# Attention kernel on one core: queries held once in steps of 28, and 112 rows of scores in place of 128

## The reference

```python
x = x + attention(layernorm(x))     # 16 heads of 128, 4 key/value heads, wq, wk, wv, wo
x = x + int8_linear(layernorm(x))   # weights and activations rounded to 8 bits, plus bias
# in attention, for each head:
scores = q @ k.T / sqrt(128)
mask = (k_pos <= q_pos) & ((k_pos < 4) | (k_pos >= q_pos - 31))
attn = softmax(where(mask, scores, lowest))
out = attn @ v                      # then @ wo.T
```

## Time and profile before

| | |
|---|---|
| median of 3 runs | 605.4 us (604.79 to 605.9) |
| profiled execution | 607.0 us, of which its span is 605.1 us |
| mean granted TensorE clock in it | 0.989 of full speed |
| busy in the span | PE 98%, DVE 89%, ACT 66%, POOL 52% |
| matmul instructions | 7556, as many weight loads |

### The profile page before, as it was taken

How to read it: one execution, slowest core, us unless ns; L and a number is a source line. 1 busy time by engine, 2 the same in 40 slices (tenths; PEclk the granted TensorE clock), 3 DMA queues, 4 the chain that set the end, 5 groups by cost and what they waited for, 6 DMA issues and landing times.

```text
span 605.1 us, 18063 instructions
## 1 busy us (share of the span) xinstructions
PE 593.6 (98%) x7556; PEld 524.7 (87%) x7556; DVE 536.3 (89%) x1072; ACT 401.0 (66%) x633; POOL 313.6 (52%) x310
## 2 busy tenths in 40 slices
PE   8999999999999999999999999999999999999995
PEld 7779888898988989888898988989898898988983
DVE  7899999898988979899898989979899898879987
ACT  7898665676666666666667566567666666666673
POOL 2155364555646455564646647455564645646473
PEclk8899999999999999999999999999999999999997
DMA  8748042150604316060250604216060330505001
GB/s 305 236 89 192 2 110 51 61 116 19 159 15 94 69 38 140 19 134 25 72 105 20 157 19 105 56 42 135 20 140 2 92 68 36 125 19 121 21 3 52
DMA packets 36272, 49.69 MB, mean 82 GB/s; under 512 B 2784, under 2 KB 22240, under 8 KB 36192
## 3 DMA queue, kind: packets, MB, share of 16 engines
q1 hardware_dynamic: 36048, 48.41, 32.6%
q10 hardware_dynamic: 144, 0.13, 0.1%
HBM read 35.42 MB, written 12.58 MB: 79 GB/s over the span
## 4 chain that ended last, share of the span: by engine, by line
PE 92%; DVE 5%; ACT 1%; issue 1%; DMA 0%; POOL 0%; DVEq 0%; POOLq 0%
PE ps L416 27%; PE ps L538 26%; PE ps L447 8%; PE ps L395 7%; PE ps L384 6%; PE ps L491 5%; PE ps L521 5%; PE ps L520 5%; PE ps L372 1%; PE ps L584 1%; PE ps L553 1%; DVE Qs L1070 1%; PE ps L569 1%; DVE pool L1097 0%; DMA X<-in_L_attn_x 0%
## 5 line engine op out<-in xcount | busy, mean ns | idle before, releaser
L416 PE MATMUL ps<-xT,WqT 128*128 128x256 f16 x1536 | 181.6, 275 | 1.0 <-DVE Qs L1070 0.7
L538 PE MATMUL ps<-WoT,pool 128*128 128x256 f16 x1440 | 167.3, 273 | 0.2 <-DVE pool L1097 0.2
L416 PEld LDWEIGHTS ps<-xT,WqT 128*128 128x128 f16 x1536 | 148.3, 99 | 18.6 <-DVE Qs L1070 1.0
L538 PEld LDWEIGHTS ps<-WoT,pool 128*128 128x128 f16 x1440 | 138.4, 98 | 15.4 <-DVE pool L1097 0.3
L1504 POOL TENSOR_TENSOR small<-E,rr 128x576 f32<-128x576 f32 x64 | 73.7, 1152 | 109.5 <-DVE rr L1092 109.3
L892 ACT ACTIVATE pool<-ps 128x512 f16<-128x512 f32 x128 | 70.2, 594 | 82.0 <-PE ps L521 82.0
L818 ACT ACTIVATE Qs<-ps 128x576 f16<-128x576 f32 x128 | 82.7, 646 | 43.7 <-PE ps L416 43.7
L1510 POOL TENSOR_TENSOR PP<-small,PP 128x576 f16<-128x576 f32 x64 | 82.0, 1282 | 52.6 <-ACT PP L879 52.6
L1070 DVE TENSOR_TENSOR Qs<-ps,Qs 128x576 f16<-128x576 f32 x128 | 92.8, 728 | 4.0 <-ACT Qs L818 4.0
L1493 POOL TENSOR_TENSOR Sm<-Sm,mx 128x576 f32<-128x576 f32 x64 | 73.7, 1152 | 36.1 <-DVE mx L1083 34.7
L1097 DVE SCALAR_TENSOR_TENSOR pool<-ps,pool 128x512 f16<-128x512 f32 x128 | 82.3, 681 | 0.2
(11 more groups left out here) (134 smaller groups left out, 893.5 us busy)
## 6 DMA issues: line engine op xcount, KB each, us to landing
values<-Vn SPq DMA_DIRECT2D x32, 256.0 KB, 2.0
VW<-values SPq DMA_DIRECT2D x16, 480.0 KB
big<-values SPq DMA_DIRECT2D x16, 480.0 KB
X<-in_L_attn_x SPq DMA_DIRECT2D x16, 256.0 KB, 8.4
VW<-values SPq DMA_DIRECT2D x16, 240.0 KB
big<-values SPq DMA_DIRECT2D x16, 240.0 KB
out<-pool SPq DMA_DIRECT2D x15, 256.0 KB, 6.0
big<-in_L_attn_wq SPq DMA_DIRECT2D x4, 512.0 KB, 8.0
```

The lines of the kernel that those rows point to most:

```text
L416: a = pe.matmul(banks[BANK_Q[f]][:, j * 256:j * 256 + 256], WqT[:, k, wl, h * 128:h * 128 + 128], xT[:, b % 2, k, xl, :], start=(n == 1), ...
L538: a = pe.matmul(out_view(b, t), OT[:, p, ol, h, t * 128:t * 128 + 128], WoT[:, 4 * g + h, wl, :], start=first, stop=(end and g == KV - 1), ...
```

## The change

Queries are held once. `Qs` has 4 x 256 columns per part in place of 9 x 128, in the order step, head, query. Step 0 keeps 32 queries (128 columns), steps 1 to 8 have 28 queries (112 columns) each. The scores of steps 1 to 8 take 112 columns of weights and give 112 rows; the transposes of `PP` take 112 rows and give 112 columns (`step_rows`). The transposes run from step 0 up, and no longer from step 8 down.

The views by which ACT and DVE write `Qs` now hold steps 1 to 8 of two heads: 2 x 8 x 28 = 448 elements. Step 0 has another length, and is written by an instruction of its own for all four heads (4 x 32 = 128 elements, reading both PSUM banks), once in a unit on ACT and once on DVE, behind the second half's. It has its own semaphores, `qs_h` and `qs_l`, and new waits: ACT's waits for `q_low(u, 0)`; `q_low(u, 1)` waits for ACT's; and each place where PE waits for `q_l` before it writes a query bank or reads `Qs` also waits for `qs_l`. The first warm-up matmuls are spread over the bank's 512 columns.

```diff
-        Qs = sb("Qs", [128, 2, 2, NT * 128], F16)
+        Qs = sb("Qs", [128, 2, 2, 4 * T], F16)
...
         def q_views(p, f):
-            src = bass.AP(ps, 512 * BANK_Q[f], [[4096, 128], [256, 2], [STEP, NT], [1, 32]])
-            dst = [bass.AP(Qs, ((p * 2 + l) * NT * 128) + 64 * f, [[4 * NT * 128, 128], [32, 2], [128, NT], [1, 32]])
+
+            src = bass.AP(ps, 512 * BANK_Q[f] + 32, [[4096, 128], [256, 2], [STEP, NT - 1], [1, STEP]])
+            dst = [bass.AP(Qs, (p * 2 + l) * 4 * T + 128 + 2 * STEP * f, [[16 * T, 128], [STEP, 2], [4 * STEP, NT - 1], [1, STEP]])
                    for l in range(2)]
             return src, dst
+
+        def q_first_views(p):
+
+            src = bass.AP(ps, 512 * BANK_Q[0], [[4096, 128], [256, 4], [1, 32]])
+            return src, [Qs[:, p, l, 0:128].rearrange("p (h q) -> p h q", h=4) for l in range(2)]
...
             def q_fill(u, f):
...
                     pe.wait_ge(q_l, 2 * (u - 1) + f + 1)
+                    pe.wait_ge(qs_l, u)
...
             def scores(u):
...
                 pe.wait_ge(q_l, 2 * u + 2)
+                pe.wait_ge(qs_l, u + 1)
...
-                            a = pe.matmul(banks[BANK_S[c]][:, (s - s0) * KEYS:(s - s0 + 1) * KEYS],
-                                          Qs[:, p, ql, s * 128:s * 128 + 128], Kw[:, b % 2, g, kl, w, :],
+                            a = pe.matmul(banks[BANK_S[c]][0:rows, (s - s0) * KEYS:(s - s0 + 1) * KEYS],
+                                          Qs[:, p, ql, 4 * q0_of(s):4 * q0_of(s) + rows], Kw[:, b % 2, g, kl, w, :],
...
             def p_transpose(u):
...
-                for s in reversed(range(NT)):
-                    a = pe.transpose(v[:, :, STEP * s:STEP * s + 32], PP[:, p, s].rearrange("p l k -> p (l k)"), idh[:, :])
+                for s in range(NT):
+                    rows = step_rows(s)
+                    a = pe.transpose(v[:, :, q0_of(s):q0_of(s + 1)], PP[0:rows, p, s].rearrange("p l k -> p (l k)"),
+                                     idh[0:rows, 0:rows])
...
             def ffn_weights():
...
                 pe.wait_ge(q_l, 2 * 9 + 1)
+                pe.wait_ge(qs_l, 10)
...
             def q_high(u, f):
...
                 act.activation(dst[0], src, ACT.Copy).then_inc(q_h, 1)
+                if f:
+                    src, dst = q_first_views(u % 2)
+
+                    act.wait_ge(q_l, 2 * u + 1)
+                    act.activation(dst[0], src, ACT.Copy).then_inc(qs_h, 1)
...
             def q_low(u, f):
                 src, dst = q_views(u % 2, f)
                 dve.wait_ge(q_h, 2 * u + f + 1)
+                if f:
+
+                    dve.wait_ge(qs_h, u + 1)
                 dve.tensor_tensor(dst[1], src, dst[0], ALU.subtract).then_inc(q_l, 1)
+                if f:
+                    src, dst = q_first_views(u % 2)
+                    dve.tensor_tensor(dst[1], src, dst[0], ALU.subtract).then_inc(qs_l, 1)
```

More of the change, by code:

```diff
@@ L38, in q0_of, with step_rows @@
     return 0 if s == 0 else STEP * s + 4
+def step_rows(s):
+    return 4 * (q0_of(s + 1) - q0_of(s))
 def output_pieces(j):
@@ L158, in build @@
         k_l, v_l, q_l = sem("k_l"), sem("v_l"), sem("q_l")
+        qs_h, qs_l = sem("qs_h"), sem("qs_l")
         s_m, s_mx, p_r = sem("s_m"), sem("s_mx"), sem("p_r")
@@ L504, in pv @@
                     pe.wait_ge(q_l, 2 * (NU - 1) + j + 1)
+                    pe.wait_ge(qs_l, NU)
                 elif u > NU - 3:
@@ L622, in _ @@
             pe.wait_ge(cst_ok, 3)
-            for _ in range(13):
-                pe.matmul(banks[BANK_S[0]][:, 0:128], small_ones[:, :], small_ones[:, :], start=True, stop=True)
+            for i in range(13):
+                pe.matmul(banks[BANK_S[0]][:, i % 4 * 128:i % 4 * 128 + 128], small_ones[:, :], small_ones[:, :], start=True, stop=True)
             scale_sums("k")
@@ L1617, in constants @@
         k0 = STEP * max(s - 1, 0)
-        for i in range(32):
-            q = STEP * s + i
+        n = step_rows(s) // 4
+        for i in range(n):
+            q = q0_of(s) + i
             keys = list(range(4)) + list(range(k0, k0 + 60))
@@ L1622, in constants @@
                 if k <= q and (c < 4 or (k >= 4 and k >= q - WIN + 1)):
-                    m[i::32, s, c] = 0.0
+                    m[i:4 * n:n, s, c] = 0.0
     eye = np.eye(128, dtype=np.float32)
```

## The result

The changed kernel takes 645.69 us (median of 6 runs, 645.16 to 646.54) against 605.65: 1.0657 of the time before, with a 95% interval of 1.064 to 1.0674. That is 40.0 us more; forecast were 33.8. The profiled execution has a span of 644.3 us.

The account below looks back on a forecast made before the run. PE, busy 98% of the span, was taken as the bound. Loads +28.3, transposes -3.4, waits +10.7 and overlap -1.8 gave +33.8 us on the profiled 607.0, 640.8; against the median 639.2, rounded 639, range 608 to 648.

Parts of the forecast that it names:

- the case that came: Scores of steps 1 to 8: a 112-column load takes 48 ns, 639 us in total, own range 632 to 648; chance 0.58.
- the load of 112 columns stays quick: Rival on the scores: narrower loads stay quick or hidden, slower through the waits alone, 612.7 us; chance 0.22.
- the float32 speed: Rival on the scores: 112-column loads are as slow as float32 loads, 95 ns, giving 708 us; chance 0.11.
- the change doesn't shorten the transposes: Rival on PE's transposes: something else sets their pace, +3.4 us on any case; no chance of its own.
- The scores' loads: Scores of steps 1 to 8: a matmul starts every 48 ns and not every 29, 1536 times, +28.3 us.
- the halving itself: Score loads: float16 taken at half float32's 109 ns load time, as on the moving side, so 48 ns for 112 columns.
- The transposes: PE's transposes of steps 1 to 8 move 112 columns in place of 128, -3.4 us; 0 if their loads became slow.
- The waits: PE stalls in prologue, unit 9 and epilogue, +10.7 us, less 1.8 for slower scores of units 0 to 3 falling into them.
- my bound of 14: Upper bound in us on PE's stalls from the new waits; the lower bound was 4.
- the granted clock: In the long stall TensorE's clock might fall to 1.2 GHz, twenty-four fills taking 2.62 us longer; inside the range, no own chance.
- Places: PE's stalls: scores of unit 1, fills of units 3, 4, 5, 6 and 63, column sums; largest over 4 us, before unit 4.
- ACT and DVE: Three instructions for two per unit: over 64 units +3.5 us on ACT, -2.6 on DVE, both hidden in the loop.

Follow-up runs that it names:

- experiment 4: The kernel before, with score matmuls of steps 1 to 8 loading only 112 of their 128 weight columns, old waits kept: 639.37 us (1.0559).
- experiment 5: The kernel before, with only the longer waits of the query fills and column sums, no instruction added: 616.45 us (1.021).
- experiment 3: experiment 2 with transposes of 128 columns again, probabilities landing at wrong queries: 605.48 us (0.9998 of before).
- experiment 6: The changed kernel with step 0 written by half and without qs_h, qs_l and their waits, 112-column loads kept: 636.72 us (1.0518).
- experiment 2: experiment 1 with step 0 written by half, each half for its own two heads, without qs_h, qs_l and their waits: 602.53 us (0.9955 of before).
- experiments 7 to 9: The kernel before, with score loads of steps 1 to 8 cut to 127, 96 and 64 of 128 columns: 649.36, 628.71 and 622.46 us.
- experiment 7: The kernel before, with score loads of steps 1 to 8 cut to 127 of 128 columns: 649.36 us.
- experiment 1: The changed kernel with score loads of 128 columns again, the 16 extra rows masked, new waits kept: 617.65 us (1.0194 of before).
- the square: Four kernels, new waits or step 0 by half: with 112-column loads 645.69 and 636.72 us, with 128-column loads 617.65 and 602.53.
- experiment 10: experiment 2 with queries held once in the order query, head, so writes and the transposes' moving reads have a stride of 4: 647.28 us (1.0688).

## Why the prediction was right, and where its sizes were off

**Direction and mechanism.** Right: both costs, the slower load and the new waits, are where they were put, and experiments 4 and 5 show each alone. The 645.7 lie in the range of 608 to 648, near its upper end, and in the 632 to 648 of the case that came. Of the rivals, "the load of 112 columns stays quick" (612.7) is refuted by experiment 4, and so is the float32 speed (708); that the change doesn't shorten the transposes is refuted by experiment 3.

**The scores' loads: +28.3 forecast, +34.2 measured** (experiment 6 against 2; 33.9 in experiment 4). This is the step that was mis-sized, and it makes up nearly the whole of the 6 us between 639.2 and 645.7. I halved the float32 pace, 109 ns, and took the result, 48 ns, as the time from matmul to matmul. The rate was right: the records of experiments 7 to 9 give about one column per cycle, by which 112 take an estimated 47 ns. But from start to start it is 51 ns. I had let the 2 ns overhead of quick loads stand for a slow one; it is 4 to 5. At 127 columns, 53 ns of load make 58. Behind the halving itself stood one row of the moving side and none of a load; that it came out was partly luck. The Trainium skill, "TensorE: Matmul & The Clock Gate", section "Weight-path perf modes", by which the quick load needs 128 weights, agrees with experiment 7, where 127 lose it. By the Trainium skill, "TensorE: Matmul & The Clock Gate", section "LDWEIGHTS", an estimate for 112 columns would be 93 ns. These runs have a score matmul every 51 ns with such a load in float16, so here the measurement decides against it.

**The transposes: -3.4 forecast, -2.95 measured** (experiment 3). That their load stays quick with 112 rows is shown by its 97 ns.

**The waits: +10.7 - 1.8 = +8.9 forecast, +9.0 measured** (experiment 6 against the changed kernel). The net is right, its two parts are not, and that they cancel is luck. Beside quick loads the waits cost 15.1 us, above my bound of 14, and 6.2 of it, not 1.8, vanish beside slow ones. What I left out of the price is the granted clock, which I had named as a mere addition inside the range: some 2.9 us by the windows above. What I left out of the overlap is that slower scores also shorten waits behind the prologue: the column sums at unit 9 wait 1.6 us in experiment 1 and 0.75 in the changed kernel. Of experiment 1, who waited for whom on PE:

```profile
PE ps L638 <- DVE Qs L1102: 1.6, 1, 1.6
```

The profile of experiment 1 also shows a second fall of the clock, at the fill of unit 3, which that of the changed kernel does not:

```profile
32.42 2.66 PE L430 MATMUL ps<-xT,WqT 128*128 128x256 f16 x12 [2.02 <-DVE Qs L1099]
```

Its windows of PE around this fall and around the fill of unit 4, which starts at 44.99:

```profile
32.00:33.00 1.00, 0.58 (x4) 0.76 1.01 199
...
35.00:36.00 1.00, 1.00 (x11) 0.54 0.56 120
...
46.00:47.00 1.00, 1.00 (x12) 0.58 0.06 16
...
49.00:50.00 1.00, 1.00 (x5) 0.71 0.00 0
```

Each of the two lasts 3.4 us, with PE at work, so together they cost 3.4 us where the one fall of the changed kernel costs 2.9: that is 0.5 of the 6.2. The waits for `Qs` make 1.9 more of it in the profiled executions (11.3 us in experiment 1 less 1.6 in experiment 2, against 9.1 in the changed kernel less 1.3 in experiment 6). The rest stays open. Some of it may be the clock near the start, which was low for some 3.4 us in the profiled execution of experiment 1 and for 6.8 in that of experiment 6, and not in the other two of the square. All four executions of experiment 1 have a mean granted clock of 0.984 to 0.987 and all six of the changed kernel one of 0.990 to 0.993; which falls come again in each is not known.

**Places.** The scores of unit 1 wait 1.18 us, 0.63 and 0.6 forecast; 1.93 us before the fill of unit 3 and 3.44 before that of unit 4 were forecast as 2 and 4; 0.64 for unit 6 as 0.7; 1.15 for unit 63 as 1.2; 0.75 for the column sums as 1.3. Unit 5's 0.7 did not come as a named wait in the changed kernel; it came with 0.58 in experiment 1.

**ACT and DVE.** 540 and 271 ns on ACT (539 and 269 forecast), 601 and 280 on DVE (588 and 240), and hidden in the loop as put: the profile lists no wait of PE for them between 120 and 600 us. **Sum** by measured terms: 34.2 - 2.95 + 9.0 = 40.2 us against 40.0. This adds no evidence, since the terms are differences along one chain of runs, from 605.48 over 602.53 and 636.72 to 645.69.

## What to carry to other kernels

Before cutting a stationary operand to the columns that are needed, keep it at 128: load the neighbours' columns and mask the rows that they give, and cut only the moving side. This is shown beside 64 moving columns; whether longer moving sides would cover the slow load no run here shows. When a piece of work is folded into one instruction across two buffers, ask of each wait on it which place in a hand-written order had relied on one buffer being free earlier; in a steady loop it can be free of cost and in the prologue cost 2% of the kernel. And a long stall of TensorE is priced with the slower clock that may follow it: behind 3.44 us without work that was some 2.9 us here.

## What the runs showed that I had not expected

- A load of 127 columns takes 42 ns more than one of 128 by its record, and 1536 of them 44 us. A load of 64 columns is still slower than a full one (113 against 98 ns), and beside 64 moving columns the pair still takes some 40 ns.
- An f16 tile written with a stride of 4 elements costs ACT 1319 ns for 512 elements and DVE 1307, about twice the adjacent write.
- Moving columns read with a stride of 4 elements go at half pace too. The timeline of experiment 10:

```profile
303.64 1.08 PE L505 MATMUL ps<-idh,PP 128*128 128x128 f16 x9
304.54 2.80 PE L553 MATMUL ps<-WoT,pool 128*128 128x256 f16 x24
```

 0.90 us for nine transposes, where adjacent columns took 0.45.
- In the changed kernel the granted clock fell to 1.2 GHz during the long stall and stayed there for 5.8 us of uninterrupted work. In experiment 1, after as long a stall, it fell only 1.2 us after work had begun again, and was back 3.4 us later. A stall of 2.02 us was followed by a fall there, stalls of 1.93 us in the changed kernel and 2.04 in experiment 5 were not.
- Outside the stalls too the clock differs between executions: the fill of unit 0 in the profiled execution of before, and in that of the changed kernel:

```profile
13.76 5.12 PE L416 MATMUL ps<-xT,WqT 128*128 128x256 f16 x24
```

```profile
13.50 2.78 PE L430 MATMUL ps<-xT,WqT 128*128 128x256 f16 x24
```

 The 24 matmuls are the same, but before ran them at half clock, 2.3 us longer. The change does spread the warm-up matmuls ahead of them, but the profiled executions of experiments 4 and 6, which have that too, were at half clock there as well. That this comes and goes with the execution fits the kernel before, whose mean granted clock was 0.989 to 0.997 in its executions. So the spans' difference, 644.3 - 605.1 = 39.2 us, understates what the loop and the stalls cost in these two traces, and the terms above are taken from the timed runs.
